# A mixture-of-experts stage with its tiles taken in pairs: weights standing and loaded at each place

## What is computed

```python
    x = x + tanh(g_xattn[0]) * L0_xattn(layernorm(x), ctx, ctx, mask)
    x = x + tanh(g_ffn[0]) * L0_ffn(layernorm(x), ...)          # the experts, below
    x = x + tanh(g_xattn[1]) * L1_xattn(layernorm(x), ctx, ctx, ...)
    x = x + tanh(g_ffn[1]) * L1_ffn(layernorm(x), ...)

    # L0_ffn: xt are the tokens, E = 8 experts, TOPK = 2
    scores = softmax(xt @ gate_w.T + gate_b)
    top_w, top_i = top_k(scores, 2)
    def expert(w1e, b1e, w3e, b3e, w2e, b2e):
        h = silu(xt @ w1e.T + b1e) * (xt @ w3e.T + b3e)
        return h @ w2e.T + b2e
    y = einsum('etd,te->td', outs, gate_dense)
    z = silu(xt @ ws1.T + bs1) * (xt @ ws3.T + bs3) @ ws2.T + bs2
    return y + z
```

## Time and profile before

| | us |
|---|---|
| median of 3 runs | 638.63 (636.67 to 639.14) |
| span of the profiled execution | 657.9 |
| TensorE busy in it | 607.1 |
| VectorE, ScalarE, GpSimd busy | 443.4, 363.6, 250.0 |
| front and tables, until the first tile's transposes | 211.3 |
| expert stage, until its last copy to `yg` | 185.0 |
| late part | 261.6 |

### The profile page before, as it was taken

One profiled execution on the slowest core, in us unless ns is written; L12 is line 12 of the kernel. 1 busy time (PEld: TensorE's weight loads), 2 busy tenths in 40 slices (PEclk: granted clock), 3 DMA queues, 4 the chain that ended last, 5 costly groups with the idle time before them and its releaser, 6 DMA issues.

```text
span 657.9 us, 12684 instructions
## 1 busy us (share of the span) xinstructions
PE 607.1 (92%) x3562; PEld 498.5 (76%) x3562; DVE 443.4 (67%) x1321; ACT 363.6 (55%) x806; POOL 250.0 (38%) x315
## 2 busy tenths in 40 slices
PE   8889999888986999999999999699879989999997
PEld 6667777776755788888888888586757867877886
DVE  3988888864653666666666663467876796866755
ACT  5687778855532555555555543155654674674643
POOL 4345564434352336232323236567442732200000
PEclk9899999988898999999999999899999999999999
DMA  6335664454063953333333317532111331100000
GB/s 199 126 126 180 220 204 160 164 167 143 25 256 120 321 162 106 105 106 105 105 107 105 106 57 260 204 117 71 49 49 48 101 108 48 49 1 32 33 33 33
DMA packets 46657, 77.53 MB, mean 118 GB/s; under 512 B 7604, under 2 KB 31615, under 8 KB 46335
## 3 DMA queue, kind: packets, MB, share of 16 engines
q1 hardware_dynamic: 38521, 57.55, 26.3%
q0 software_dynamic: 7344, 19.14, 8.7%
q10 hardware_dynamic: 726, 0.02, 0.1%
HBM read 44.52 MB, written 32.17 MB: 117 GB/s over the span
## 4 chain that ended last, share of the span: by engine, by line
PE 52%; DVE 18%; issue 9%; ACT 7%; DMA 4%; POOL 4%; another core or an unknown queue 4%; SPq 1%; ACTq 0%; DVEq 0%; POOLq 0%
PE bank L1162 11%; PE bank L1164 10%; PE bank L1163 10%; PE bank L1602 5%; PE bank L1623 3%; PE bank L1624 3%; PE bank L1464 2%; PE bank L1455 2%; DMA rows_by_expert<-n,pos 2%; DVE xa L2077 2%; DVE st L2086 2%; PE bank L1562 2%; DVE sl L2155 1%; DVE xa L2138 1%
## 5 line engine op out<-in xcount | busy, mean ns | idle before, releaser
L582 POOL TENSOR_TENSOR yg<-yg,b 128x256 f32<-128x256 f32 x71 | 52.3, 737 | 115.7 <-ACT yg L699 115.7
L2038 DVE TENSOR_TENSOR hb<-bank,b 128x512 f32<-128x512 f32 x71 | 49.1, 692 | 59.4 <-PE bank L1164 59.1
L536 POOL DMA_INDIRECT rows_by_expert<-n,pos x64 | 65.6, 1025 | 61.2 <-DVE pos L1890 44.7
L1602 PE MATMUL bank<-n4Th,wint 128*128 128x512 f32 x192 | 74.6, 409 | 5.5 <-DVE sl L2155 4.1
L624 POOL DMA_INDIRECT yr<-expert_out,out_row x64 | 66.7, 1042 | 20.4 <-issue 17.4
L699 ACT ACTIVATE hTh<-bank 128x256 fp32r<-128x256 f32 x71 | 27.3, 384 | 82.0 <-PE bank L1464 82.0
L1602 PE MATMUL bank<-n4Tl,wint 128*128 128x512 f32 x192 | 71.9, 395 | 0.0
L699 ACT ACTIVATE g3h<-sl 128x512 fp32r<-128x512 f32 x60 | 37.8, 631 | 45.5 <-DVE sl L2155 32.0
L1162 PE MATMUL bank<-w13h,xTh 128*128 x142 | 56.4, 397 | 0.2 <-DVE xTl L2045 0.2
L1164 PE MATMUL bank<-w13h,xTl 128*128 x142 | 56.0, 394 | 0.0
L1163 PE MATMUL bank<-w13l,xTh 128*128 x142 | 55.8, 393 | 0.0
(11 more groups left out here) (299 smaller groups left out, 1787.6 us busy)
## 6 DMA issues: line engine op xcount, KB each, us to landing
xg<-rows_by_expert SPq DMA_DIRECT2D x71, 128.0 KB, 2.1
expert_out<-yg SPq DMA_DIRECT2D x71, 128.0 KB, 1.7
stage<-in_wexp SPq DMA_DIRECT2D x24, 256.0 KB
x_shared<-x SPq DMA_DIRECT2D x8, 512.0 KB
xa<-x_shared SPq DMA_DIRECT2D x4, 1024.0 KB
out<-ost SPq DMA_DIRECT2D x8, 512.0 KB, 2.6
xin<-in_x SPq DMA_DIRECT2D x7, 512.0 KB, 5.1
wint<-in_wint POOLq DMA_DIRECT2D x3, 768.0 KB, 10.7
```

Of the source, the lines that this page charges most:

```text
L536: pool.indirect_dma_start(out=xs, out_offset=bass.IndirectOffsetOnAxis(ap=pos[p][:, k, j:j + 1], axis=0), in_=n2[p][:, j, :], in_offset=No ...
L582: pool.tensor_tensor(yg[s], yg[s], b2[:, bass.ds(e, 1), :].rearrange("p a d -> p (a d)"), ALU.add)\
L1602: last = mm(bank[:, 2 * (m % 2) + w, :], wt[:, k, m * P:(m + 1) * P], part[c][:, k, :], start=(q == 0 and k == 0), stop=(q == 1 and k == K ...
L2038: tt(hb[p], bank[:, p, :], b13[:, bass.ds(e, 1), :].rearrange("p a n -> p (a n)"), ALU.add)\
```

## The change

The expert stage takes 40 places in place of 71 tiles: NP = 31 pairs (256 rows of one expert) and NS = 9 single tiles (128 rows), in the fixed order `KINDS`: 13 pairs, then nine times pair, pair, single.

- In a pair the first layer's *weights* stand and 256 token columns move: 4 pieces x 2 x 3 = 24 matmuls. The result is already transposed, so the two transposes of `hid` and the copies behind them fall away, and the bias is one number per partition: ACT's silu takes it with the bank, DVE adds the other in the same instruction as the product. A single tile keeps the old form.
- The first layer's weights are no longer kept. For each place SP loads the expert's two pieces (512 KB) from HBM to one of three `wraw`, ACT copies the high parts (128x1024) to one of two `wph`, DVE makes `wpl`. In the front only the second layer's piece is left of each expert (`expert_high`, `expert_low`, `load_expert`), and it is loaded a step earlier.
- `xg`, `yg`, `xTh`, `xTl`, `hTh`, `hTl` and the add on POOL are of twice the width for a pair; `yg` has three buffers in place of four.
- The tables have one more level of small products and sums (which tiles go in pairs, which are left over). Each place reads its row and its expert from them: one `value_load` each for the weights, the tile and the store on SP, and for a pair one on ACT too.
- Loads of the last weights of the model (`wint`) and of rows for the late part move from the stage's head into it, `b13` too. Elsewhere long helpers are called in halves, in the same order.

Cut to its core:

```diff
-            for t in range(NT - 1):
-                if t + 8 < NT:
-                    load_tile(t + 8, t % 4)
-                store_tile(t, t % 4)
+            for u in range(NU):
+                if u + 4 < NU:
+                    load_weights(u + 4)
+                if u + 5 < NU:
+                    load_tile(u + 5)
+                if u:
+                    store_tile(u - 1)
...
+            def weights_high(u):
+                act.wait_ge(sem(f"stage_in{u % 3}"), 16 * (EARLY[u % 3] + u // 3 + 1))
+                if u >= 2:
+                    act.wait_ge(sem("hm_done"), u - 1)
+                copy(wph[u % 2], wraw[u % 3]).then_inc(sem("high_done0"), 1)
...
+            for u in range(NU + 2):
+                if u + 1 < NU:
+                    weights_high(u + 1)
+                if 0 < u <= NU and not pair(u - 1):
+                    high_of(u - 1)
+                if u < NU:
+                    silu_of(u)
+                if u < NU and pair(u):
+                    high_of(u)
+                if u >= 2 and not pair(u - 2):
+                    out_copy(u - 2)
+                if 0 < u <= NU and pair(u - 1):
+                    out_copy(u - 1)
+                if u + 2 < NU:
+                    rows_high(u + 2)
...
+                if pair(u):
+                    for m in range(4):
+                        o = bank[:, 2 * p + m // 2, m % 2 * P2:(m % 2 + 1) * P2]
+                        for k in range(KD):
+                            wh, wl = (w[p][:, k, m * P:(m + 1) * P] for w in (wph, wpl))
+                            n = slice(k * P2, (k + 1) * P2)
+                            last = three(o, wh, wl, xTh[p][:, n], xTl[p][:, n], k == 0, k == KD - 1)
+                        if m == 1:
+                            last.then_inc(sem("ha_done"), 1)
...
+            for u in range(NU + 2):
+                if u < NU:
+                    hidden(u)
+                if u + 1 < NU:
+                    experts[u + 1] = expert_of(u + 1)
+                if u >= 2 and not pair(u - 2):
+                    outp(u - 2, experts[u - 2])
+                if 0 < u <= NU and not pair(u - 1):
+                    th(u - 1)
+                if 0 < u <= NU and pair(u - 1):
+                    outp(u - 1, experts[u - 1])
+                if u + 2 < NU:
+                    tx(u + 2)
...
+            for u in range(NU + 1):
+                if u + 1 < NU:
+                    weights_low(u + 1)
+                if u and not pair(u - 1):
+                    hidden_low_of(u - 1)
...
+                if u < NU:
+                    gated(u)
+                if u < NU and pair(u):
+                    hidden_low_of(u)
+                if u + 2 < NU:
+                    rows_low(u + 2)
+                if u < NU and not pair(u):
+                    gated_single(u)
```

More of the change, by code:

```diff
@@ L18 @@
 NT = 2 * T // P + NE - 1
+NP, NS = 31, 9
+NU = NP + NS
+EARLY = [2 + len(range(c, NE, 3)) for c in range(3)]
+KINDS = "P" * (NP - 2 * NS) + "PPS" * NS
+assert len(KINDS) == NU and KINDS.count("S") == NS
+P2 = 2 * P
+assert 2 * NP + NS == NT
 SPARE = NE * RC
@@ L1031, in late_high @@
                 copy(lhh[:, m, :], lsil[m % 2]).then_inc(sem("hh_done"), 1)
+            first, second = range(2), range(2, GT)
             late_silu(0, 0)
@@ L1522, in _, with outp @@
-            step2(Turn(0, 4, NT), experts, x=False, h=False, ahead=False)
-            step2(Turn(0, 4, NT + 1), experts, x=False, h=False, hd=False, ahead=False)
+            def outp(u, e):
+                p = u % 2
+                pe.wait_ge(sem("hTl_done"), u + 1)
+                if u >= 2:
+                    pe.wait_ge(sem("y_done"), u - 1)
+                tiles = 2 if pair(u) else 1
+                for j in range(tiles):
+                    for k in range(KD):
+                        wh, wl = (w[:, bass.ds(e, 1), k * D:(k + 1) * D].rearrange("p a n -> p (a n)") for w in (w2h, w2l))
+                        s = slice((tiles * k + j) * P, (tiles * k + j + 1) * P)
+                        last = three(bank[:, 6 + p, j * D:(j + 1) * D], hTh[p][:, s], hTl[p][:, s], wh, wl, k == 0, k == KD - 1)
+                last.then_inc(sem("y_mm_done"), 1)
@@ L2073, in x2 @@
                 for k in ks:
-                    for j in range(GT):
+                    for j in tiles:
                         if k:
@@ L2270, in _ @@
                 if more:
-                    x2(u + GB, (0,))
+                    x2(u + GB, (0,), first)
+                if more:
+                    x2(u + GB, (0,), second)
                 hidden3(b, 0, 4)
```

1141 lines of the change are left out of this document (686 added, 455 removed).

## The result

| | us |
|---|---|
| before, median of 4 runs | 637.65 (633.96 to 639.14) |
| after, median of 4 runs | 647.37 (645.79 to 649.04) |
| ratio | 1.0146, 95% interval 1.0115 to 1.0177 |
| forecast | 634.0, range 622 to 653 |

The kernel after is 9.7 us slower. The forecast was 3.6 us faster; the time lies inside its range, on the side to which I had given 0.37.

A forecast was written before the change was run, and what follows sets the result against it. TensorE was taken to bound the expert stage at 2.54 us a tile, and only partly the front. Front -8 and stage +3.5 gave -4.5 on 638.6: 634 us, range 622 to 653 (own range 628 to 641).

The forecast's parts named there:

- TensorE in a pair: Expert stage: TensorE takes 4.70 us a pair, against 5.08 for two tiles, by saving the four transposes of `hid`.
- The two-queue loop: Expert stage, pairs: the loop across ScalarE and VectorE from `wph` to the next takes 4.68 us, tying with TensorE's 4.70.
- The load of the expert number: Expert stage, behind `wpl` and `wph`: hidden in pairs, cost 0; otherwise 0.34 us in the loop, kept for the range.
- first rival: Expert stage: loop longer than TensorE's pass, expert-number load and wide parts uncovered; +17, 651 us; chance 0.28.
- The single tiles: Expert stage, pair-pair-single groups: 14.0 us for five tiles that took 12.7; nine groups' singles lose 12 us.
- second rival: Expert stage: GpSimd's add gets in VectorE's way, 40 x 0.4 = +16, 650 us; chance 0.07.
- Head and end of the stage: Expert stage from 210.1 takes 189 us, ending at 399 against 396.3: +3; last GpSimd add +0.5.
- 5.9 to the first result, 12 x 4.67: Head of the expert stage: 5.9 us to the first result, then 12 steps of 4.67 us.
- DMA in the stage: Expert stage: about 46 MB in 189 us, 244 GB/s, a share of 0.7; nothing to pay while it flows.
- The front: Before the expert stage: fewer weight copies, subtractions and loads, and stalls and low clock gone, give -8 us (-3 to -12).
- The late part: After the expert stage: same instructions, loads and ScalarE's unnamed wait may fall otherwise; 0, +-5 us.
- the stage ends between 392 and 405: End of the expert stage: the forecast is wrong if it ends before 392 or after 405 us.

The follow-up runs named there:

- after_again: The kernel after, timed and profiled once more with no edit: 646.2 us, ratio 1.014 to the kernel before.
- four_raw: Kernel after with third wide-part buffers, wide parts in the gaps, single's transposes earlier, loads reordered, fourth raw-weight buffer: 625.4 us, ratio 0.980 to the kernel before.
- narrow_add: Kernel after with GpSimd's bias adds on 8 columns in place of 256 in each half: 642.2 us, ratio 1.008 to the kernel before.
- loads_only: Kernel after with only the load edits (four raw buffers, first rows earlier, late loads parted), its own engine order: 661.8 us, ratio 1.015 to the kernel before.
- before_third: The kernel before, profiled again with no edit: span 634.6 us.
- th_ahead: Kernel after with a single place's two transposes ahead of the next hidden layer instead of behind it: 670.9 us, ratio 1.053 to the kernel before.

## Why the prediction was wrong, by its own steps

- **TensorE in a pair, 4.70.** 0.05 too low, and of little weight: the first matmuls of two pairs are 4.75 apart, in after_again and in four_raw alike.
- **The two-queue loop, 4.68.** Right: 4.70 from one `wph` to the next in the pairs, 0.05 below TensorE's pass. The terms too: `wph` 1.05 to 1.07 (1.06), `wpl` 1.21 to 1.23 where GpSimd is away (1.24). ScalarE through one pass of the kernel after:

```profile
225.11 1.06 ACT L785 ACTIVATE wph<-wraw 128x1024 fp32r<-128x1024 f32 x1
226.06 0.84 ACT L1021 ACTIVATE hb<-bank,b13c 128x256 f32<-128x256 f32 x2
228.34 0.63 ACT L785 ACTIVATE hTh<-hb 128x512 fp32r<-128x512 f32 x1 [1.44 <-DVE hb L2282]
...
229.83 1.06 ACT L785 ACTIVATE wph<-wraw 128x1024 fp32r<-128x1024 f32 x1
```

  The tie with TensorE was real.
- **The load of the expert number, 0 in a pair.** Right for the kernel after: behind `wph` and `wpl` there is no idle time in its pairs. So the pairs' part of the first rival ("the loop is longer than TensorE's pass", 651) is out, though its time was near. The mechanism is not far away, though: in narrow_add VectorE is idle by "issue" for 0.18 to 0.32 us behind `wpl` in four of the pairs, and these take 4.96 to 5.10.
- **The single tiles, 14.0 a group.** The step that failed first: it left GpSimd's add out and was short in the pass behind a single place. A group took 14.7 in the mean of eight groups. 0.5 of the 0.7 is GpSimd's add (narrow_add, 14.2), which is the second rival's mechanism at a quarter of its price: it falls on the wide part in some passes only, and not on all 40, and on the product of the single place. The other 0.2 is in the pass behind a single place: 4.94 with narrow adds, where I had 4.75 (5.15 with the adds as they are). There ScalarE's load of the expert number follows a short copy and stands uncovered, and VectorE waits for what comes after it. The forecast names this load in its walk of the pass but gives no terms for its 4.75, so that how much of it is in there can't be told; that the load is on the path behind a single place was the other half of the first rival, at 0.7 a group. 9 x 0.7 = 6.4 us. From the kernel after, ScalarE, then VectorE:

```profile
304.29 0.84 ACT L1021 ACTIVATE hb<-bank,b13c 128x256 f32<-128x256 f32 x2 [0.34 <-issue]
```

```profile
304.98 0.88 DVE L2282 SCALAR_TENSOR_TENSOR hb<-bank,b13c,hb 128x256 f32<-128x256 f32 x2 [0.53 <-ACT hb L1021]
```

- **Head and end of the stage, +3.** The second that failed. "5.9 to the first result, 12 x 4.67" holds no load and no clock. In after_again, TensorE at the stage's head:

```profile
190.57 1.29 PE L1629 MATMUL bank<-ident,xg 128*128 128x128 f32 x8 [2.48 <-DMA xg<-rows_by_expert]
192.73 0.55 PE L1316 MATMUL bank<-xTh,wph 128*128 128x256 f32 x1 [0.87 <-DVE xTl L2268]
193.09 0.41 PE L1317 MATMUL bank<-xTl,wph 128*128 128x256 f32 x1
193.30 0.41 PE L1318 MATMUL bank<-xTh,wpl 128*128 128x256 f32 x1
...
198.91 0.28 PE L1317 MATMUL bank<-xTl,wph 128*128 128x256 f32 x1
199.02 0.28 PE L1318 MATMUL bank<-xTh,wpl 128*128 128x256 f32 x1
```

  After a wait of 2.48 us for rows and 0.87 for their low part, the first place's 24 matmuls are 0.21 apart (granted clock 0.50, that is 1.2 GHz) in place of the 0.12 of the second place's, +2.2 us. ScalarE has a table load (`ACT_TABLE_LOAD`) of 1.28 us ahead of the first silu, and later waits 1.53 for the raw weights of place 2. The first two passes take 14.1 where 9.4 were counted: 4.8 us. How the 4.8 divide was not priced by a run; four_raw, which asks for these loads in another order, takes 9.35.
- **DMA in the stage, 0.7 and 244 GB/s.** Right as a mean (0.65 to 0.81, 204 to 271 GB/s), and no bound in the groups of the kernel after (loads_only). At the head it was busier than that (a share of 0.86 from 194 to 198 us, and 402 GB/s from 198 to 202, at whose end place 2's weights landed). "Nothing to pay while it flows" was true behind the head, and of this order only.
- **The front, -8.** In direction right, too large: by step 5 the kernel after is 4.9 us ahead (5 were counted) and by step 6 7.7 (8.1), but 0.9 is lost again behind it, so that the steps gave 6.8 where 8.1 were counted, and the tables and the first tile's rows took 2.6 where 0.5 were. The wait of 1.84 for `logitT` belongs to the kernel (2.17 in before_third, behind a `w13h` copy that waits 4.21 for its load; none in after_again); the low clock behind it, 1.3 us of the sum, does not (the granted clock is 1.00 from 120 to 150 us in before_third). "That span is 3% above the median; terms of this size need no scaling" was the sentence that hid this: what had to be asked was not how to scale but which rows belong to that execution alone. The unnamed waits and some of the clock did.
- **The late part, 0.** Right (-0.5).
- **The sign "the stage ends between 392 and 405"** was set in absolute time and is void: it ended at 390.6, outside it, since the front ended 20 us earlier than in the profile I had, of which only 4.2 are the change's.

Put together, the stage misses by 11 us: 6.4 of groups and 4.8 of head less some tenths at its end; the front and the way to the first tile by 3.8. Less the 0.5 of the late part that is the 14.3 us between -4.5 and +9.8. What the walk of a group got wrong was what runs beside it: it gave each instruction the duration that it has alone. The deeper reading is in four_raw: the walk was of the order as it stood, and took 14.0 for what the engines can do, while 12.3, with TensorE full, can be had with the same instructions.

## What to carry to other kernels

Work put into a loop over two queues costs by its place more than by its amount: with the two wide parts (1.06 and 1.22 us a place) ahead of the chain to the next matmul a group takes 14.7 us, and with the same parts in the gaps in which ScalarE and VectorE wait for each other, the single place's product ahead of them and the loads asked for in time, it takes 12.3, at which TensorE is full. These moves were made together; only the buffers, the transposes and the loads were also tried alone, and none of them gained anything alone. Before an order is changed, look at what the moved instruction waits for in its new place: the same move of two transposes was part of a gain of 6.7 us in one order and a loss of 24 in the other, and each mended order has a next bound (here the moment at which loads are asked for). And before counting on stalls of one profile, compare it with a second of the same kernel: here two profiles of one kernel lie 23 us of 658 apart.

## What the runs showed of the hardware

- A VectorE instruction with two inputs in SBUF and a GpSimd instruction that reads SBUF shut each other out for about the rest of the one that came first: `wpl` 2.26 us in place of 1.22, `shift_one` 1.5 in place of 0.50, adds of 1.75 in place of 1.29. Where VectorE was on the path this cost 0.5 us in each group of three, where it had slack nothing that could be told.
- Two executions of the same kernel, 652.6 and 634.6 us: the longer one has waits for releases without a name (14.0, 6.2, 3.7, 3.0 us), which come back at the same places in other long executions, and a mean granted clock of 0.98 in place of 0.99 to 1.00.
- After an idle stretch of 3.7 us TensorE's granted clock was 0.62 over the next 4.5 us (th_ahead, from 289.5 us), between its levels of 1.2 and 2.4 GHz: the matmuls were 0.12 apart at first and then 0.21.
